# The bias of a recurrence set into PSUM by ScalarE ahead of the products, in place of a sum behind the transposition

## The reference

```
x = x + attention(x, cond)          # 16 heads of 32, causal, one extra key and value from cond
xw = x @ Wx + b                     # over all 512 positions
h = tanh(h @ Wh + xw[t])            # t = 0 .. 511, one after another; h is 8 x 512
x = x + all h
```

## Time and profile before

| | us |
|---|---|
| median of 3 runs | 1801.43 (1799.96 to 1805.03) |
| the profiled execution: its time | 1800.27 |
| its span, by the profile | 1798.5 |
| PE busy | 1634.6 (91%) |
| DVE busy | 888.8 (49%) |
| ACT busy | 709.9 (39%) |

### The profile page before, as it was taken

The page is one execution under the profiler, slowest core; times in us unless marked ns, Lnnn a source line. Parts: engine busy times, 40 slices in busy tenths (PEclk is TensorE's granted clock), DMA queues, the critical chain, the costliest instruction groups (busy, mean ns, idle before and its releaser), DMA issues.

```text
span 1798.5 us, 67877 instructions
## 1 busy us (share of the span) xinstructions
PE 1634.6 (91%) x29292; PEld 1378.1 (77%) x29292; DVE 888.8 (49%) x2986; ACT 709.9 (39%) x2205; POOL 149.6 (8%) x248
## 2 busy tenths in 40 slices
PE   5788889898999998999999999898998998999997
PEld 4777778786878787877878788686886887887876
DVE  4444435454545455555555565465655574222222
ACT  2444545444344444444444444444444453111111
POOL 0110100010000100010111100011001000000000
PEclk8988989999999999999999999998998999999999
DMA  7744536443435464554545566554565561100000
GB/s 253 188 146 138 145 118 186 131 129 108 127 111 155 109 160 119 141 150 126 138 128 154 131 160 159 137 151 132 139 157 136 153 152 38 27 16 17 26 16 21
DMA packets 228442, 221.67 MB, mean 123 GB/s; under 512 B 22952, under 2 KB 187048, under 8 KB 227632
## 3 DMA queue, kind: packets, MB, share of 16 engines
q1 hardware_dynamic: 211568, 175.86, 37.0%
q0 software_dynamic: 16576, 41.46, 8.1%
HBM read 141.45 MB, written 75.76 MB: 121 GB/s over the span
## 4 chain that ended last, share of the span: by engine, by line
PE 72%; DVE 9%; DMA 7%; issue 5%; ACT 4%; SPq 2%; POOL 1%; DVEq 0%; POOLq 0%; ACTq 0%
PE rec L926 24%; PE turned L849 8%; PE dense L381 7%; PE dense L382 6%; PE dense L383 6%; PE pv L862 4%; PE scores L841 4%; PE scores L926 3%; PE dense L897 3%; DVE pre L753 3%; ACT hist L594 3%; DMA msk<-mask 2%; DMA x_dram<-x1nat 2%; PE pv L880 2%; DVE probs L688 1%
## 5 line engine op out<-in xcount | busy, mean ns | idle before, releaser
L926 PE MATMUL rec<-wh,hist 128*8 128x128 f32 x14336 | 483.7, 275 | 62.9 <-ACT hist L594 56.6
L926 PEld LDWEIGHTS rec<-wh,hist 128*8 128x8 f32 x14336 | 355.2, 94 | 145.5 <-ACT hist L594 103.9
L552 ACT ACTIVATE probs<-probs,nmax 128x128 f32<-128x128 f32 (+3 forms) x512 | 287.9, 563 | 220.6 <-DVE nmax L688 211.7
L594 ACT ACTIVATE hist<-pre 128x32 f32<-128x32 f32 x512 | 131.9, 258 | 576.7 <-DVE pre L763 340.4
L688 DVE CUSTOM_DVE_ANT_0 probs<-scores,msk,nimg 128x128 f32<-128x128 f32 (+3 forms) x512 | 276.2, 544 | 58.4 <-PE scores L841 56.5
L753 DVE STREAM_TRANSPOSE pre<-rec 128x128 f32<-128x128 f32 x448 | 141.3, 315 | 319.8 <-PE rec L926 317.4
L849 PE MATMUL turned<-ident,probs 128*128 128x128 f32 x1280 | 241.0, 288 | 1.9 <-DVE probsT L697 0.9
L841 PE MATMUL scores<-kq 96*128 96x128 f32 (+3 forms) x512 | 203.8, 403 | 37.7 <-DVE nmax L688 23.7
L849 PEld LDWEIGHTS turned<-ident,probs 128*128 128x128 f32 x1280 | 145.3, 141 | 65.3 <-issue 55.2
L697 DVE COPY probsT<-turned 128x128 f32<-128x128 f32 (+3 forms) x256 | 124.7, 487 | 97.0 <-PE turned L849 95.8
L559 ACT COPY probsT<-turned 128x128 f32<-128x128 f32 (+3 forms) x256 | 108.1, 422 | 147.9 <-PE turned L849 146.7
(11 more groups left out here) (119 smaller groups left out, 2293.1 us busy)
## 6 DMA issues: line engine op xcount, KB each, us to landing
kq<-kq_dram SPq DMA_DIRECT2D x96, 320.0 KB, 5.6
kq<-kq_dram SPq DMA_DIRECT2D x96, 256.0 KB, 4.7
kq<-kq_dram SPq DMA_DIRECT2D x96, 192.0 KB, 3.7
kq_dram<-qs_hi SPq DMA_DIRECT2D x128, 128.0 KB, 2.5
kq_dram<-ks_hi SPq DMA_DIRECT2D x128, 128.0 KB, 2.4
kq<-kq_dram SPq DMA_DIRECT2D x96, 128.0 KB, 2.6
xin<-x SPq DMA_DIRECT2D x32, 256.0 KB, 3.2
kq_dram<-qs_lo SPq DMA_DIRECT2D x64, 128.0 KB, 2.4
```

Source lines behind the costliest of these rows:

```text
L552: act.activation(probs[:, g % PROBS, 0:n], probs[:, g % PROBS, 0:n], ACT.Exp, scale=-1.0, bias=nmax[:, e, h:h + 1], accum_out=rowsum[:, e, ...
L594: act.activation(hist[:, g // HALF % 2, :, :, g % HALF], pre[:, :, 0:B], ACT.Tanh).then_inc(h_ready, 1)
L926: last = pe.matmul(d[Q * j:Q * j + B, 0:P], hist[:, before // HALF, f, :, before % HALF], wh[:, f, P * j:P * j + P], start=f == 0 and not ...
```

## The change

A tile `bxrows` is made once in the setup: DVE spreads `bx` over `pre` (128 x 128) and transposes it, so that it has the layout of a step's bank. In the last block, ACT copies `bxrows` into the bank of step t = g + 2 behind the tanh of step g. All products of the tail step add to it (`start=False` throughout), and line 918 waits on the new `bias_set` in place of `rec_turned`. The transposition signals `pre_ready` itself; the sum of line 756 is gone.

```diff
+            def set_bias(t):
+                if t == FIRST:
+                    act.wait_ge(bx_turned, 1)
+                    act.wait_ge(shifted_ready, HEADS)
+                elif t == FIRST + 1:
+                    act.wait_ge(rec_turned, FIRST)
+                else:
+                    act.wait_ge(pre_ready, t - 1)
+                act.copy(rec_bank(t)[:, 0:P], bxrows[:]).then_inc(bias_set, 1)
...
                     act.activation(hist[...], pre[:, :, 0:B], ACT.Tanh).then_inc(h_ready, 1)
+                    if g >= FIRST - 2 and g + 2 < S:
+                        set_bias(g + 2)
...
+            dve.wait_ge(setup_loaded, SETUP_LOADS)
+            dve.tensor_copy(pre[:], bx[:].unsqueeze(2).broadcast_to([P, C, Q])).then_inc(bx_spread, 1)
+            dve.wait_ge(bx_spread, 1)
+            dve.transpose(bxrows[:], pre_all).then_inc(bx_turned, 1)
+            dve.wait_ge(bx_turned, 1)
...
                     dve.wait_ge(rec_ready, g + 1)
-                    dve.transpose(pre_all, rec_bank(g)[:, 0:P]).then_inc(rec_turned, 1)
-                    dve.wait_ge(rec_turned, g + 1)
                     if b == BLOCKS - 1:
-                        dve.tensor_tensor(pre[:, :, 0:B], pre[:, :, 0:B],
-                                          bx[:].unsqueeze(2).broadcast_to([P, C, B]), ALU.add).then_inc(pre_ready, 1)
+                        dve.transpose(pre_all, rec_bank(g)[:, 0:P]).then_inc(pre_ready, 1)
                         if s == 0:
                             set_out(r, 1)
                     else:
+                        dve.transpose(pre_all, rec_bank(g)[:, 0:P]).then_inc(rec_turned, 1)
+                        dve.wait_ge(rec_turned, g + 1)
...
-                        pe.wait_ge(rec_turned, g - 1)
+                        pe.wait_ge(bias_set, g - FIRST + 1)
...
-                                          start=f == 0, stop=False)
+                                          start=False, stop=False, skip_group_check=True)
```

More of the change, by code:

```diff
@@ L251, in attention_recurrence @@
         imgT = sb("imgT", [P, C, B])
+        bxrows = sb("bxrows", [P, P])
         dense = [ctx.enter_context(nc.psum_tensor(f"dense{i}", [P, BANK], F32)) for i in range(2)]
@@ L343, in attention_recurrence @@
         rec_turned = sem("rec_turned")
+        bx_spread = sem("bx_spread")
+        bx_turned = sem("bx_turned")
+        bias_set = sem("bias_set")
         pre_ready = sem("pre_ready")
@@ L372, in heads_tile @@
             return kq_tiles[:, group % TILES, 0:HC * n].rearrange("p (j n) -> p j n", j=HC)
+        FIRST = (BLOCKS - 1) * P
         def rec_bank(t):
@@ L926, in _ @@
                             last = pe.matmul(d[Q * j:Q * j + B, 0:P], hist[:, before // HALF, f, :, before % HALF],
-                                             wh[:, f, P * j:P * j + P], start=f == 0 and not tail, stop=f == C - 1)
+                                             wh[:, f, P * j:P * j + P], start=f == 0 and not tail, stop=f == C - 1,
+                                             skip_group_check=tail)
                     last.then_inc(rec_ready, 1)
```

## The result

Over 19 runs of each kernel, the changed one takes 1783.25 us (median, 1776.18 to 1801.54), the kernel before 1802.32 (1797.73 to 1807.91). The ratio is 0.9902, 95% interval 0.9882 to 0.9922: 17.7 us less (14 to 21), where 26.1 were forecast.

The account below looks back on a forecast made before the run. It took the tail as bound by a ring of dependent work (transposition, sum, tanh, line 926), 2.02 us a turn. 26.3 + 0.45 - 0.61 = 26.1 us less, 1775.3; own range 1771 to 1780, all cases 1770 to 1788.

Parts of the forecast that it names:

- rival 1: Tail, PE line 926 behind the closer 918 costs 0.10 us a turn: 14.5 us less, 1787; chance 0.11.
- What the sum's absence is worth in a turn: Tail's dependent chain: the sum's start to tanh's start, 0.225 us, leaves each turn; 117 full gains make 26.3 us.
- The distances behind an `out`: Tail, behind 8 `out` steps: transpositions 2.46 us apart, a distance of PE's own, so the gain is 0.
- Steps 416, 448, 480: Tail, where line 644's copy must end before line 918: gain 0.15 us each, together 0.45.
- The copy: ACT's tail copies into PSUM: 0.30 us each, `bias_set` 0.43 us early or more, so cost 0.
- The setup: DVE between `wproj_lo` and `xT_lo`: spread, transposition and two hops add 0.61 us, bounds 0 and 0.7.
- TensorE at less reserve: Tail, line 926 with loader idle time down from 0.36 to about 0.14 us: cost 0, bounds 0 and 0.10 a step.
- Rival 2: Tail: line 926 can't load before line 918 has ended, gain 0.08 us a turn, 9.2 less, 1792; chance 0.03.
- rival 4: Tail: tanh starts no earlier, or a hold-up cancels the gain, so no change, 1801; chance 0.02.
- Rival 3: Tail: ACT's PSUM write holds up PE's writes to the other bank, 12 to 24.5 us more, 1813 to 1826; chance 0.02.
- What the chain would show: Tail between `out` steps: chain still through 926, 753, 594; PE 918 on ordinary turns would mean the prediction is wrong.
- The attention, that was to stay within 1 us: Attention, its order unchanged: a change of more than 1 us would mean the prediction is wrong.

Follow-up runs that it names:

- no_copy: Changed kernel without the bias in the last 128 steps: no copy by ScalarE, first products overwrite again, sum stays away; 1785.2 us, ratio 0.9887.
- sum_and_copy: Changed kernel with the sum put back behind the transposition and the copies kept, so the bias is added twice; 1802.32 us, ratio 0.9994.
- narrow: Changed kernel with x1's products over 32 moving columns in place of 128, as many instructions; 1780.76 us, ratio 0.9880.
- half_products: Changed kernel with half of x1's products left out, 96 TensorE instructions a turn in place of 128; 1768.06 us, ratio 0.9800.
- after_again: The changed kernel unaltered, run once more for a second profile; 1781.44 us, ratio 0.9875.
- before_waits: Kernel before with 16 long-met waits ahead of line 918 in each of the last 128 steps, which became 8 instructions; 1825.43 us, ratio 1.0120.
- before_half: Kernel before with half of x1's products (line 918) left out; 1800.7 us, ratio 0.9995.
- four_ahead: Changed kernel with x1's products made for four steps at once and x1's columns laid out earlier, 80 TensorE instructions a turn; 1771.23 us, ratio 0.9803.

## Why the prediction was right, and where it was not

The direction, the mechanism and the turn were right; the sum was too large by 8 us (26.1 against 17.7), and the measured time lies in the range given for all cases, not in the forecast's own (1771 to 1780). That it lies in the wider one is luck in part: the range reached to 1788 to make room for rival 1, which didn't occur, and what did occur was in no part of it.

- **What the sum's absence is worth in a turn.** Forecast 0.225, found 2.018 - 1.797 = 0.22. The hop from DVE to ACT is 0.035 as assumed.
- **The distances behind an `out`.** Forecast 0, found 0: 2.46 before and after. They belong to TensorE.
- **Steps 416, 448, 480.** 0.15 each was reckoned; 2.94 became 2.69, 0.25 each, 0.3 us more in all. The copy starts 0.08 ahead of the transposition's end, the far end of what the prediction allowed, and takes 0.38 instead of 0.42.
- **The copy.** Taken at 0.30, found 0.29; its cover held. no_copy and sum_and_copy show it as free.
- **The setup.** 0.61 forecast, 0.59 found.
- **TensorE at less reserve, the step that failed.** The prediction asked only whether the array and the weight loads had room, took 0 between the bounds 0 and 0.10 a turn, and noted 0.14 us of idle loader. The array did have room: from first load to transposition it is still 1.14 in the median, and narrow shows that more room leaves the turn and the stalls as they are. What had none was the supply of TensorE's own instructions, which the prediction didn't price at all. The trace of before had it: four turns late by 1.4 us in sum, with TensorE idle and nothing awaited, and 128 loads and matmuls a turn could be counted in the earlier trace rows (the 32 products of each line there are 16 in the code). At 4.04 us for 256 instructions the supply just sufficed; at 3.59 it fell behind in 20 to 33 turns for 8.2 to 11.6 us. 26.1 + 0.3 - (11.6 - 1.4) = 16.2 and, with 8.2, 19.6: around the 17.7 measured.
- **The rivals.** Rival 1 gave 1787, nearer to the 1783 found than the 1775 forecast, but not by its mechanism: the turns without a stall keep 1.13 to 1.16 and not the 1.23 that it wanted. Rival 2 would have needed 1.94 in every turn, rival 4 2.02. Rival 3 is refuted by no_copy.
- **What the chain would show.** The forecast said that between the `out` steps it would run through 926, 753 and 594 as before, and that line 918 on it would mean that the prediction is wrong. It doesn't run so: the view follows TensorE alone, the products of line 943 with it, as the idle time of 0.14 before line 951 is too small to be noted. The sign was badly chosen for a reserve of this size. From 1598.5 to 1604.5 us:

```profile
by line: PE scores L951 30.8%; PE scores L943 29.1%; PE rec L951 22.6%; PE rec L943 17.9%
```

  That the ring still sets the turn is shown by half_products and narrow, with 0.6 us of reserve and the same 1.79 to 1.80.
- **The attention, that was to stay within 1 us.** It didn't: step 384 was reached 6.3 us later than before in the first profile and 5.0 us earlier in the second. Its time moves with the granted clock (see after_again), by more between two profiles of one kernel than the sign allowed, so it tells nothing of the change.

Left open: what decides when a packet is started (0.9 to 2.6 us after the load 128 places before the stalled one), how much of the delay comes from the other transfers, and why before_waits loses more than its rate would make one expect.

## What to carry to other kernels

When a ring of dependent work gets shorter, everything that the engines consume per turn is asked for faster, their instructions too. Count an engine's instructions in a turn, and look for idle time that has no releaser and comes at a fixed count of instructions: some of it in the kernel before, hidden or nearly so, is a price that grows with the shorter turn (here from 1.4 us to between 8 and 12). Where it comes up, fewer and wider instructions (here the part that doesn't depend on the ring, made for four steps at once) give back what the shorter ring should have brought. The test that settles it is the time from the landing of an instruction packet to the end of each such idle time: here it was 1.2 to 1.6 us every time.

## What the runs showed of the hardware

- TensorE's stream of small f32 products ran at 256 instructions in 4.8 us or more (half_products, before_half, four_ahead) with a single late turn, by 0.16 us, with 1.4 us of lateness in 127 turns at 4.04, and with 8 to 12 us at 3.59. With 8 satisfied waits among each 136 instructions it was 22.7 us at 3.93 (before_waits), so the rate isn't all. In the eight traces at 128 instructions a turn every stall of 0.25 us or more ended 1.20 to 1.62 us after a packet of 16 KB had landed.
- ScalarE writing 128 x 128 f32 into one bank of PSUM doesn't slow TensorE's products into another: they take 1.07 with it and without. The copy takes 0.284 to 0.297 us beside them.
- In the first profile of the changed kernel the granted clock was 0.50, the 1.2 GHz level, from 1528 to 1531 us, after TensorE had waited 2.15 us, up to 1527.64, for the first columns of x1; line 943's first run of 32 took 1.76 us, and step 384 came 1.5 us late. In the kernel before the clock stayed at 1.00 behind the same wait of 2.14 us. All this is ahead of the block's first transposition. The row of the changed kernel (columns as in the earlier trace rows):

```profile
1528.00:1531.00 3.00, 3.00 (x64) 2.50 (x60) 0.00 (x0) 0.00 (x0) 0.00 (x0) 0.50 0.24 93
```
